# A clustering layer with a 1x1 convolution: the convolution's products in halves of 256 columns, and a changed order in the fourth slot and the last ones

## The chip, the cores and the metric

The kernel runs on one core of one Trainium2 chip. The metric is the device time of one execution in microseconds (us). Three runs of the kernel before took 430.16, 430.51 and 432.31 us; their median is 430.51 us.

## The reference

The input x is 8 x 512 x 32 x 48, that is 8 batches of 512 channels and 1536 tokens. W is 512 x 512, and there are 40 centroids of 512 channels. All is float32.

```
xn  = x / max(norm(x over channels), eps)       cn = centroids / max(norm, eps)
idx = argmax over the 40 centroids of <xn, cn>  onehot = one_hot(idx, 40)
sum_x = onehot^T x ;  count = sum(onehot)       mean = sum_x / max(count, 1)
delta = mean[idx] - x
alpha = exp(-mean over channels of delta^2)
y     = x + alpha * delta
out   = relu(W y + b)
```

The means are taken within a batch, so a batch's tokens must all be assigned before its first delta can be made.

## The kernel before

The work is cut into 24 units of 512 tokens, three per batch. A unit g passes through these steps, each on the engine named:

- **TensorE (PE)**: `similarities` (centroids by x), `transpose_sims`, `sum_clusters` (one-hot by transposed x), `transpose_onehot`, `add_halves`; `gather(g, h)` multiplies means by one-hot and gives the mean of each token in two halves of 256 channels; `sum_squares(g)` sums delta squared over channels into the bank `al` with a matrix of ones; `convolve(g, o)` makes 128 output channels (o = 0 to 3) into one bank of `main` (bank o % 2).
- **VectorE (DVE)**: `transpose_half` transposes x (tile `xs` into `xt`), two instructions per unit; `delta(g, h)`, `add_squares`, `fold`, `low_sum`, `scale(g, h)` (delta times alpha). For the last units also half of y and of its low part.
- **ScalarE (ACT)**: `square`, `move_upper`, `high_sum`, `exp`, `high_half`, `relu(g, o)` (empties the bank of `main`), and small copies.
- **GpSimd (POOL)**: `y_half` (adds x) and `low_half` (y minus its rounded part).

The convolution is made exact enough by splitting both factors. y = YH + YL, W = WH + WL, all of type fp32r, and three products are summed: WH·YH, WH·YL, WL·YH. So `convolve(g, o)` makes 4 values of k times 3 products = 12 matmuls, each with 128 x 128 weights and 512 moving columns, all added into one bank. Each matmul loads its weights first; the load is an instruction of its own, in the profile as PEld. Of the 96 pairs (g, o) two (g = 0, o = 0 and 1) are made elsewhere (L863 to L868 and L909 to L913), which leaves 94 calls.

The order of every engine is written out by hand, and semaphores tie the engines together. A pass through the loop `for g in range(PARTS, UNITS)` is called a slot here: in slot g the unit g gets its delta and its sum of squares, unit g-1 its alpha, y, YH and YL, and unit g-2 is convolved. The slots run from g = 3 to 23; the slot g = 3 is the fourth unit's ("fourth slot"). `beside` is true while a next batch is prepared beside the current one (g < 21); in slots 21 to 23 it is false. After the loop units 22 and 23 are convolved.

Waits that matter below:

- `convolve(g, o)` waits for `relu_done >= 4 g + o - 1` (L818), that is for the relu that emptied its bank; for o = 0 also for YH and YL of the two halves (L822, L823), the second of them only at k = 2.
- `sum_squares(g)` waits for `high_sum(g)` and `low_sum(g)` (L804, L805); `low_sum` itself waits for `high_sum`, and that for `fold` (L538).
- `gather(g, 0)` waits for the last sum of `add_squares(g-1)`, `gather(g, 1)` for `delta(g, 0)` (L791, L796).
- SyncE's queue is in order too: `load_xs(g)` waits for the transposes of unit g-2 (L212), and the loads and stores behind it wait with it (L233 to L246).

Of the kernel before, what the change touches and what calls it, by code (L numbers as in the profile page):

```python
# [16 lines left out]
KC = C // P  # L17
UNIT = 512
PARTS = HW // UNIT
# [46 lines left out]
def build(nc, x, cent, w, bias, out):  # L66
# [3 lines left out]
    with ctx:  # L70
# [16 lines left out]
        YH = [sb(f"yh{j}", [P, KC, UNIT], F32R) for j in range(2)]  # L87
        YL = [sb(f"yl{j}", [P, KC, UNIT], F32R) for j in range(2)]
# [214 lines left out]
        def _(dve):  # L303
# [6 lines left out]
            def transpose_half(g, h):  # L310
                M = C // BLK
                blocks = slice(h * M // 2, (h + 1) * M // 2)
                if h == 0:
                    dve.wait_ge(xs_in[g % 2], 16 * Q * ((g - PARTS) // 2 + 1))
                    dve.wait_ge(c_done, g - PARTS + 1)
                last = v_.transpose(XT[:, g % PARTS, :, :].rearrange("p t (m j) -> p m t j", j=BLK)[:, blocks, :, :],  # L316
                                    XS[g % 2][:, blocks, :])
                if h == 1:
                    last.then_inc(tr_done, 1)

            def best_sims(b):
                dve.wait_ge(simT_done, b + 1)
                wait(dve, oh_done, b)
                v_.tensor_reduce(best[:, :], simT, AXIS_X, ALU.max).then_inc(arg_step, 1)
# [44 lines left out]
            def delta(g, h):  # L369
                dve.wait_ge(gat_done, 2 * g + h + 1)  # L370
                if g >= 2:
                    wait_low(dve, g - 2, h)
                v_.tensor_tensor(Z[g % 2][:, pair(h), :], banks(g, h)[:, :, :],  # L373
                                 X[g // PARTS % 2][:, pair(h), span(g)], ALU.subtract).then_inc(z_done, 1)
# [14 lines left out]
            def low_sum(g):  # L389
                dve.wait_ge(sh_done, folded(g))  # L390
                v_.tensor_tensor(SHL[LOW:P, :], al[0:LOW, :], SHL[0:LOW, :].bitcast(F32), ALU.subtract  # L391
                                 ).then_inc(sl_done, 1)

            def scale(g, h):
                dve.wait_ge(exp_done, g + 1)
                z = Z[g % 2][:, pair(h), :]
                v_.tensor_tensor(z, z, alpha(g).unsqueeze(1).to_broadcast([P, 2, UNIT]), ALU.mult  # L397
                                 ).then_inc(za_done, 1)
# [8 lines left out]
            def low_half(g, h):  # L407
                if not low_on_vector(g, h):
                    return
                dve.wait_ge(hi_done, 2 * g + h + 1)  # L410
                wait(dve, main_done, KC * (g - 1))
                v_.tensor_tensor(YL[g % 2][:, pair(h), :], Z[g % 2][:, pair(h), :],
                                 YH[g % 2][:, pair(h), :].bitcast(F32), ALU.subtract).then_inc(lo_dve, 1)
# [58 lines left out]
            parts_of_mean(1)  # L472
            fold(2)
            low_sum(2)
            transpose_half(6, 0)
            transpose_half(6, 1)
            for g in range(PARTS, UNITS):
                b, p = divmod(g, PARTS)
                beside = b + 1 < BATCH
                delta(g, 0)  # L480
                scale(g - 1, 0)
                scale(g - 1, 1)
                delta(g, 1)
                y_half(g - 1, 1)
                if beside and p < 2:
                    transpose_half(g + 4, 0)
                if beside and p == 2:
                    low_clusters(b + 1)
                    counts(b + 1)
                add_squares(g)  # L490
                if beside and p == 0:
                    transpose_half(g + 4, 1)
                fold(g)
                if beside and p == 2:
                    rest_of_mean(b + 1)
                if beside and p == 1:
                    best_sims(b + 1)
                low_half(g - 1, 1)
                low_sum(g)
                if beside and p == 1:  # L500
                    first_best(b + 1)
                    transpose_half(g + 4, 1)
                if beside and p == 2:
                    parts_of_mean(b + 1)
                    if g + 4 < UNITS:
                        transpose_half(g + 4, 0)
                        transpose_half(g + 4, 1)
            g = UNITS - 1
# [6 lines left out]
        def _(act):  # L515
# [17 lines left out]
            def move_upper(g):  # L533
                act.wait_ge(s_done, folded(g))
                a_.activation(upper_sum[:, :], al[LOW:P, :], ACT.Copy).then_inc(upper_done, 1)  # L535

            def high_sum(g):
                act.wait_ge(fold_done, folded(g))  # L538
                wait(act, one_done, g)
                a_.activation(SHL[0:LOW, :], al[0:LOW, :], ACT.Copy).then_inc(sh_done, 1)  # L540

            def exp(g):
                act.wait_ge(one_done, g + 1)
                a_.activation(alpha(g), alpha(g), ACT.Exp, scale=-1.0 / C).then_inc(exp_done, 1)  # L544

            def high_half(g, h):
                wait_y(act, g, h)
                wait(act, main_done, KC * (g - 1))
                a_.activation(YH[g % 2][:, pair(h), :], Z[g % 2][:, pair(h), :], ACT.Copy).then_inc(hi_done, 1)  # L549

            def relu(g, o):
                if g < 0:
                    return
                act.wait_ge(main_done, KC * g + o + 1)
                if o == 0:
                    wait(act, out_done[g % 2], 16 * (g // 2))
                a_.activation(OUT[g % 2][:, o, :], main[:, o % 2, :], ACT.Relu, bias=bcol[:, o:o + 1]  # L557
                              ).then_inc(relu_done, 1)
# [93 lines left out]
            high_means(1)  # L652
            move_upper(2)
            high_half(1, 1)
            high_sum(2)
            relu(0, 2)
            for g in range(PARTS, UNITS):
                b, p = divmod(g, PARTS)
                beside = b + 1 < BATCH
                relu(g - 3, 3)  # L660
                if g > PARTS:
                    exp(g - 1)
                square(g, 0)
                if beside and p == 2:
                    high_half(g - 1, 0)
                    copy_sums(b + 1)
                    evacuate_onehot(b + 1)
                    square(g, 1)
                    high_half(g - 1, 1)
                    relu(g - 2, 0)  # L670
                    scale_means(b + 1)
                    move_upper(g)
                    high_means(b + 1)
                    high_sum(g)
                    relu(g - 2, 1)
                else:
                    relu(g - 2, 0)
                    if g == PARTS:
                        exp(g - 1)
                    square(g, 1)  # L680
                    if beside:
                        copy_sims(3 * b + 3 + 2 * p)
                    high_half(g - 1, 0)
                    if beside and p == 0:
                        copy_sims(3 * b + 4)
                    if not beside:
                        relu(g - 2, 1)
                    move_upper(g)
                    high_half(g - 1, 1)
                    high_sum(g)  # L690
                    if beside:
                        relu(g - 2, 1)
                relu(g - 2, 2)
                if beside and p == 1:
                    copy_onehot(b + 1)
# [13 lines left out]
        def _(pe):  # L709
# [98 lines left out]
            def sum_squares_direct(g):  # L808
# [4 lines left out]
                                     start=(k == 0), stop=(k == KC - 1))  # L813
                last.then_inc(one_done, 1)

            def convolve(g, o, ks=range(KC)):
                if ks[0] == 0:
                    wait(pe, relu_done, KC * g + o - 1)  # L818
                rows = slice(o * P, (o + 1) * P)
                for k in ks:  # L820
                    if o == 0 and k % 2 == 0:
                        pe.wait_ge(hi_done, 2 * g + k // 2 + 1)  # L822
                        wait_low(pe, g, k // 2)  # L823
                    t_.matmul(main[:, o % 2, :], WH[:, k, rows], YH[g % 2][:, k, :], start=(k == 0), stop=False)  # L824
                    t_.matmul(main[:, o % 2, :], WH[:, k, rows], YL[g % 2][:, k, :], start=False, stop=False)  # L825
                    last = t_.matmul(main[:, o % 2, :], WL[:, k, rows], YH[g % 2][:, k, :], start=False,  # L826
                                     stop=(k == KC - 1))
                if ks[-1] == KC - 1:
                    last.then_inc(main_done, 1)

# [141 lines left out]
```

## Time and profile before

| | |
|---|---|
| median of three runs | 430.51 us |
| the profiled execution | 429.74 us, of which the span of the trace is 427.9 us |
| granted TensorE clock | 1.00 of 2.4 GHz |
| PE busy (matmuls) | 416.4 us, 97% |
| PEld busy (weight loads) | 291.1 us, 68% |
| DVE, ACT, POOL busy | 301.8, 255.1, 206.6 us |
| mean of one, DVE | transpose 1.23, delta 1.22, scale 1.21, low_half 1.37 us |
| mean of one, ACT | high_half 1.05, relu 0.68, exp 0.59, high_sum 0.59 us |
| mean of one, POOL | y_half 2.39, low_half 2.42 us |

The span runs from the first to the last instruction; 1.8 us of the execution lie around it. Rows of the trace have the start in us, the duration in us, the engine, the line, the operation, the tiles (output <- inputs) and shapes, a count of equal instructions that stand in a row, and in brackets the idle time of the engine ahead of it with what ended it. The record of a matmul is longer than the time by which the next one follows, since matmuls overlap in the array; the pace is read from the starts. "x8" rows cover eight records, and their duration is from the first start to the last end. A float32 matmul (f32, not fp32r) stands in the trace as two records, each of two passes over its columns.

### The profile page before, as it was taken

What the parts mean: (1) busy time and instruction counts of PE and PEld (TensorE: products, weight loads), DVE (VectorE), ACT (ScalarE), POOL (GpSimd) and SP (SyncE); (2) the same over time, 40 slices, a digit from 0 to 9 for tenths busy, and PEclk for the clock granted to TensorE, in tenths of its full rate; (3) what the DMA queues carried; (4) which work ended last, traced back from release to release, by engine and by line L of the source; (5) the groups of instructions that cost most, each with busy time, mean ns of one, the idle gap of its engine ahead of it and who ended that gap; (6) DMA issues with size and microseconds to landing.
All of it is one profiled execution on the core that took longest, in us unless ns stands there. A gap on an engine that the chain in (4) does not pass through costs nothing.

```text
span 427.9 us, 5755 instructions
## 1 busy us (share of the span) xinstructions
PE 416.4 (97%) x2106; PEld 291.1 (68%) x2106; DVE 301.8 (71%) x400; ACT 255.1 (60%) x351; POOL 206.6 (48%) x102
## 2 busy tenths in 40 slices
PE   7999998899999999999999999999999999999996
PEld 6744464675867757775767758777677758777785
DVE  2468977687884868678694877958685877788730
ACT  5755383665764675656755666647745657566641
POOL 2000653774563771854744853735816745324320
DMA  8997296867489393966769573983946220222213
GB/s 276 309 285 129 59 266 162 256 192 179 165 207 284 100 243 105 281 159 164 230 164 251 176 185 114 256 232 121 272 90 205 100 98 2 98 100 98 94 68 133
DMA packets 70927, 73.94 MB, mean 173 GB/s; under 512 B 2724, under 2 KB 45732, under 8 KB 70900
## 3 DMA queue, kind: packets, MB, share of 16 engines
q1 hardware_dynamic: 70900, 73.58, 61.6%
q8 instruction: 17, 0.28, 0.3%
q14 instruction: 10, 0.08, 0.1%
HBM read 48.40 MB, written 25.17 MB: 172 GB/s over the span
## 4 chain that ended last, share of the span: by engine, by line
PE 81%; DVE 10%; ACT 3%; issue 2%; DMA 2%; SPq 0%; ACTq 0%; DVEq 0%
PE main L824 17%; PE main L825 16%; PE main L826 16%; PE sump L768 10%; PE fa L728 8%; PE gat L799 5%; DVE z L397 2%; DMA x<-x 2%; DVE z L373 2%; DVE xt L316 1%; PE al L806 1%; PE fa L737 1%; PE fa L752 1%; PE main L867 1%; DVE al L383 1%
## 5 line engine op out<-in xcount | busy, mean ns | idle before, releaser
L286 POOL TENSOR_TENSOR z<-z,x 128x1024 f32<-128x1024 f32 x42 | 99.4, 2386 | 144.8 <-DVE z L397 144.8
L824 PE MATMUL main<-yh,wh 128*128 128x512 f32 x376 | 152.5, 406 | 2.9 <-ACT o L557 2.9
L826 PE MATMUL main<-yh,wl 128*128 128x512 f32 x376 | 146.7, 390 | 0.0
L825 PE MATMUL main<-yl,wh 128*128 128x512 f32 x376 | 146.7, 390 | 0.0
L293 POOL TENSOR_TENSOR yl<-z,yh 128x1024 fp32r<-128x1024 f32 x44 | 105.9, 2423 | 58.6 <-ACT yh L549 58.6
L557 ACT ACTIVATE o<-main,bcol 128x512 f32<-128x512 f32 x96 | 65.1, 682 | 70.9 <-PE main L826 70.9
L373 DVE TENSOR_TENSOR z<-gat,x 128x1024 f32<-128x1024 f32 x46 | 56.2, 1222 | 59.3 <-PE gat L799 59.3
L824 PEld LDWEIGHTS main<-yh,wh 128*128 128x128 f32 x376 | 70.6, 188 | 23.8 <-issue 4.6
L826 PEld LDWEIGHTS main<-yh,wl 128*128 128x128 f32 x376 | 70.6, 188 | 15.2
L825 PEld LDWEIGHTS main<-yl,wh 128*128 128x128 f32 x376 | 70.7, 188 | 13.9
L549 ACT ACTIVATE yh<-z 128x1024 fp32r<-128x1024 f32 x48 | 50.4, 1051 | 22.9 <-POOL z L286 21.9
L397 DVE TENSOR_TENSOR z<-z,al 128x1024 f32<-128x1024 f32 x46 | 54.0, 1213 | 3.5 <-ACT al L544 3.5
L316 DVE STREAM_TRANSPOSE xt<-xs 128x1024 f32<-128x1024 f32 x42 | 51.0, 1230 | 0.0
L728 PE MATMUL fa<-x,c_t 128*64 128x256 f32 x384 | 45.2, 383 | 0.6 <-DMA x<-x 0.3
L768 PE MATMUL sump<-xt,oh 128*64 128x512 f32 x192 | 43.6, 598 | 0.0
L728 PEld LDWEIGHTS fa<-x,c_t 128*64 128x64 f32 x384 | 26.7, 137 | 18.0 <-issue 6.9
L531 ACT ACTIVATE gat<-z 128x1024 f32<-128x1024 f32 x22 | 22.6, 1027 | 20.6 <-DVE z L373 20.6
L531 ACT ACTIVATE sq<-z 128x1024 f32<-128x1024 f32 x22 | 23.3, 1061 | 16.3 <-DVE z L373 16.3
L768 PEld LDWEIGHTS sump<-xt,oh 128*64 128x64 f32 x192 | 12.8, 136 | 25.5 <-issue 25.5
L799 PE MATMUL gat<-oht,g 128*128 128x512 bf16 x92 | 27.8, 384 | 1.1 <-DVE g L366 0.6
L387 DVE TENSOR_TENSOR al<-upper_sum,al 64x512 f32<-64x512 f32 x22 | 15.0, 680 | 10.2 <-ACT upper_sum L535 10.2
L391 DVE TENSOR_TENSOR shl<-al,shl 64x512 fp32r<-64x512 f32 x22 | 15.1, 685 | 6.8 <-ACT shl L540 6.5
(114 smaller groups left out, 335.7 us busy)
## 6 DMA issues: line engine op xcount, KB each, us to landing
x<-x SPq DMA_DIRECT2D x24, 1024.0 KB, 5.7
out<-o SPq DMA_DIRECT2D x23, 1024.0 KB, 5.6
xs<-x SPq DMA_DIRECT2D x84, 256.0 KB, 5.6
o<-w SPq DMA_DIRECT2D x1, 1024.0 KB, 12.2
out<-o SPq DMA_DIRECT2D x4, 256.0 KB, 2.1
sq<-centroids SPq DMA_DIRECT2D x2, 80.0 KB
bcol<-bias SPq DMA_DIRECT2D x1, 2.0 KB, 11.8
```

The costliest lines, as they stand in the source:

```text
L286: pool.tensor_tensor(z, z, X[g // PARTS % 2][:, pair(h), span(g)], ALU.add).then_inc(y_pool, 1)
L293: pool.tensor_tensor(YL[g % 2][:, pair(h), :], Z[g % 2][:, pair(h), :], YH[g % 2][:, pair(h), :].bitcast(F32), ALU.subtract).then_inc(lo_p ...
L316: last = v_.transpose(XT[:, g % PARTS, :, :].rearrange("p t (m j) -> p m t j", j=BLK)[:, blocks, :, :], XS[g % 2][:, blocks, :])
L373: v_.tensor_tensor(Z[g % 2][:, pair(h), :], banks(g, h)[:, :, :], X[g // PARTS % 2][:, pair(h), span(g)], ALU.subtract).then_inc(z_done, 1)
L397: v_.tensor_tensor(z, z, alpha(g).unsqueeze(1).to_broadcast([P, 2, UNIT]), ALU.mult).then_inc(za_done, 1)
L549: a_.activation(YH[g % 2][:, pair(h), :], Z[g % 2][:, pair(h), :], ACT.Copy).then_inc(hi_done, 1)
L557: a_.activation(OUT[g % 2][:, o, :], main[:, o % 2, :], ACT.Relu, bias=bcol[:, o:o + 1]).then_inc(relu_done, 1)
L728: last = t_.matmul(simP[u][NPAD * h:NPAD * (h + 1), :], cT[:, k, :], toks, start=(k == 0), stop=(k == KC - 1))
L768: last = t_.matmul(sumP[NPAD * h:NPAD * (h + 1), :], oh[:, slot(u, tile), :], XT[:, u, tile, :], start=(u == 0 and t == 0), stop=(u == PAR ...
L824: t_.matmul(main[:, o % 2, :], WH[:, k, rows], YH[g % 2][:, k, :], start=(k == 0), stop=False)
L825: t_.matmul(main[:, o % 2, :], WH[:, k, rows], YL[g % 2][:, k, :], start=False, stop=False)
L826: last = t_.matmul(main[:, o % 2, :], WL[:, k, rows], YH[g % 2][:, k, :], start=False, stop=(k == KC - 1))
```

## The change

Two things are changed.

**Halves.** In `convolve` each of the three products of a k is made as two matmuls of 256 columns with the same weights, except WH·YH of k = 0, the first into its bank, which stays 512 wide. A call then makes 1 + 2 + 2 + 3 x 6 = 23 matmuls instead of 12. No weight load is shared: each matmul has its own.

**Orders.** In slot 3: VectorE makes `delta(3, 0)` ahead of the two transposes of unit 6; ScalarE makes `relu(0, 2)` and `relu(0, 3)` ahead of `high_sum(2)` instead of behind it. In slots 21 to 23: ScalarE makes `high_sum(g)` ahead of `high_half(g-1, 1)`; VectorE makes `low_sum(g)` ahead of `low_half(g-1, 1)` (in the other slots VectorE has no `low_half`, so that edit moves nothing there).

```
             for g in range(PARTS, UNITS):
                 delta(g, 0)
+                if g == PARTS:
+                    transpose_half(g + 3, 0)
+                    transpose_half(g + 3, 1)
...
+                low_sum(g)
                 low_half(g - 1, 1)
-                low_sum(g)
...
             high_half(1, 1)
+            relu(0, 2)
+            relu(0, 3)
             high_sum(2)
-            relu(0, 2)
...
                     move_upper(g)
+                    if not beside:
+                        high_sum(g)
                     high_half(g - 1, 1)
-                    high_sum(g)
                     if beside:
+                        high_sum(g)
                         relu(g - 2, 1)
...
-                    t_.matmul(main[:, o % 2, :], WH[:, k, rows], YH[g % 2][:, k, :], start=(k == 0), stop=False)
-                    t_.matmul(main[:, o % 2, :], WH[:, k, rows], YL[g % 2][:, k, :], start=False, stop=False)
-                    last = t_.matmul(main[:, o % 2, :], WL[:, k, rows], YH[g % 2][:, k, :], start=False,
-                                     stop=(k == KC - 1))
+                    if k == 0:
+
+                        t_.matmul(main[:, o % 2, :], WH[:, k, rows], YH[g % 2][:, k, :], start=True, stop=False)
+                    else:
+                        for half in column_halves:
+                            t_.matmul(main[:, o % 2, half], WH[:, k, rows], YH[g % 2][:, k, half],
+                                      start=False, stop=False)
+                    for half in column_halves:
+                        t_.matmul(main[:, o % 2, half], WH[:, k, rows], YL[g % 2][:, k, half],
+                                  start=False, stop=False)
+                    for half in column_halves:
+                        last = t_.matmul(main[:, o % 2, half], WL[:, k, rows], YH[g % 2][:, k, half],
+                                         start=False, stop=(k == KC - 1 and half is column_halves[-1]))
```

VectorE around the start of slot 3, before: L387 and L391 are `fold(2)` and `low_sum(2)`, L316 the transposes of unit 6, L373 `delta(3, 0)`, L397 `scale(2, 0)` and `scale(2, 1)`.

```order
53 L387 TENSOR_TENSOR al<-upper_sum,al 64x512
54 L391 TENSOR_TENSOR shl<-al,shl 64x512
55 L316 STREAM_TRANSPOSE xt<-xs 128x8x4x32 x2
56 L373 TENSOR_TENSOR z<-gat,x 128x1024
57 L397 TENSOR_TENSOR z<-z,al 128x1024 x2
```

And now:

```order
53 L387 TENSOR_TENSOR al<-upper_sum,al 64x512
54 L391 TENSOR_TENSOR shl<-al,shl 64x512
55 L373 TENSOR_TENSOR z<-gat,x 128x1024
56 L316 STREAM_TRANSPOSE xt<-xs 128x8x4x32 x2
57 L397 TENSOR_TENSOR z<-z,al 128x1024 x2
```

The two transposes now stand between the delta and the scaling.

ScalarE in slot 22, before: L535 is `move_upper`, L549 `high_half`, L540 `high_sum`, L557 `relu`.

```order
272 L557 ACTIVATE o<-main,bcol 128x512
273 L535 ACTIVATE upper_sum<-al 64x512
274 L549 ACTIVATE yh<-z 128x1024
275 L540 ACTIVATE shl<-al 64x512
276 L557 ACTIVATE o<-main,bcol 128x512 x2
```

And now (the same functions stand one line lower in the changed file):

```order
272 L558 ACTIVATE o<-main,bcol 128x512
273 L536 ACTIVATE upper_sum<-al 64x512
274 L541 ACTIVATE shl<-al 64x512
275 L550 ACTIVATE yh<-z 128x1024
276 L558 ACTIVATE o<-main,bcol 128x512 x2
```

The copy that `low_sum` waits for has moved ahead of one of 1.05 us.

TensorE in one call of `convolve`, now: L832 is the wide product of k = 0, L835, L838 and L841 are WH·YH, WH·YL and WL·YH in halves.

```order
747 L832 MATMUL main<-yh,wh 128x512
748 L838 MATMUL main<-yl,wh 128x256 x2
749 L841 MATMUL main<-yh,wl 128x256 x2
750 L835 MATMUL main<-yh,wh 128x256 x2
751 L838 MATMUL main<-yl,wh 128x256 x2
752 L841 MATMUL main<-yh,wl 128x256 x2
```

Eleven of a call's twelve matmuls have become pairs.

## Rows read from the trace of the kernel before

**Rows 1.** The page's parts 1 and 4: busy time, and the chain that ended last.

```profile
PE 416.4 (97%) x2106; PEld 291.1 (68%) x2106; DVE 301.8 (71%) x400; ACT 255.1 (60%) x351; POOL 206.6 (48%) x102
PE 81%; DVE 10%; ACT 3%; issue 2%; DMA 2%; SPq 0%; ACTq 0%; DVEq 0%
```

**Rows 2.** Windows: busy time of each engine in one stretch, clock, DMA share, GB/s.

```profile
118.00:365.00 247.00, 247.00 (x1258) 173.54 (x1257) 182.08 (x219) 152.23 (x210) 141.84 (x60) 1.00 0.63 175
```

**Rows 3.** Timeline of TensorE at the end: from one row to the other are 48 matmuls.

```profile
413.44 0.39 PE L826 MATMUL main<-yh,wl 128*128 128x512 f32 x1
...
424.32 0.39 PE L826 MATMUL main<-yh,wl 128*128 128x512 f32 x1
```

**Rows 4.** Timeline of TensorE: float32 matmuls of 512 columns, bf16 transposes of 128.

```profile
37.73 3.60 PE L812 MATMUL al<-o,ones 128*128 128x512 f32 x8
41.16 3.60 PE L812 MATMUL gat<-o,ones 128*128 128x512 f32 x8
...
57.19 0.83 PE L752 MATMUL fa<-identb,oh 128*128 128x128 bf16 x12
```

**Rows 5.** Lines L825 and L799: duration of one record, min/median/max in ns.

```profile
L825 PEld LDWEIGHTS main<-yl,wh x376: 187/188/192, 57.9 to 423.9; 128*128 128x128 f32 x188
L825 PE MATMUL main<-yl,wh x376: 387/389/398, 58.1 to 424.1; 128*128 128x512 f32 x188
...
L799 PE MATMUL gat<-oht,g x92: 377/379/390, 33.4 to 393.7; 128*128 128x512 bf16 x92
```

**Rows 6.** The costliest groups: line L752; behind the bar busy us and mean ns.

```profile
L752 PE MATMUL fa<-identb,oh 128*128 128x128 bf16 x96 | 6.7, 219 | 0.0
```

**Rows 7.** Timeline of all engines at 205.4: weight loads at a convolution's start.

```profile
205.47 0.19 PEld L824 LDWEIGHTS main<-yh,wh 128*128 128x128 f32 x1
205.58 0.19 PEld L825 LDWEIGHTS main<-yl,wh 128*128 128x128 f32 x1
...
205.81 0.39 PE L825 MATMUL main<-yl,wh 128*128 128x512 f32 x1
```

**Rows 8.** The same at 88.0: a convolution's last matmul and the gather behind it.

```profile
88.01 0.39 PE L826 MATMUL main<-yh,wl 128*128 128x512 f32 x1
...
88.24 0.12 PEld L799 LDWEIGHTS gat<-oht,g 128*128 128x128 bf16 x2 [0.26 <-issue]
```

**Rows 9.** Timeline of TensorE in slot 3.

```profile
64.80 0.61 PE L799 MATMUL gat<-oht,g 128*128 128x512 bf16 x2 [0.33 <-DVE g L366]
66.58 0.50 PE L824 MATMUL main<-yh,wh 128*128 128x512 f32 x1 [1.18 <-ACT o L557]
...
81.96 0.50 PE L824 MATMUL main<-yh,wh 128*128 128x512 f32 x1 [1.76 <-ACT o L557]
```

**Rows 10.** Timeline of ScalarE in slot 3.

```profile
63.10 1.05 ACT L549 ACTIVATE yh<-z 128x1024 fp32r<-128x1024 f32 x1
65.37 0.59 ACT L540 ACTIVATE shl<-al 64x512 fp32r<-64x512 f32 x1 [1.22 <-DVE al L387]
65.86 1.25 ACT L557 ACTIVATE o<-main,bcol 128x512 f32<-128x512 f32 x2
70.22 1.06 ACT L531 ACTIVATE sq<-z 128x1024 f32<-128x1024 f32 x1 [3.11 <-DVE z L373]
```

**Rows 11.** Timeline of VectorE in slot 3.

```profile
66.71 2.37 DVE L316 STREAM_TRANSPOSE xt<-xs 128x1024 f32<-128x1024 f32 x2
69.00 1.19 DVE L373 TENSOR_TENSOR z<-gat,x 128x1024 f32<-128x1024 f32 x1
72.38 2.35 DVE L397 TENSOR_TENSOR z<-z,al 128x1024 f32<-128x1024 f32 x2 [2.19 <-ACT al L544]
```

**Rows 12.** Timeline of the SyncE queue: the loads behind the transposes of unit 6.

```profile
69.11 1.91 SPq L215 DMA_DIRECT2D xs<-x  x4
```

**Rows 13.** Timeline of TensorE in slot 21, at the end of unit 19's convolution.

```profile
376.85 0.39 PE L826 MATMUL main<-yh,wl 128*128 128x512 f32 x1
...
377.45 0.47 PE L806 MATMUL al<-shl,ones 128*128 128x512 f32 x1 [0.22 <-DVE shl L391]
```

More of the change, by code:

```diff
@@ L474, in _ @@
             low_sum(2)
-            transpose_half(6, 0)
-            transpose_half(6, 1)
             for g in range(PARTS, UNITS):
@@ L659, in _ @@
                 beside = b + 1 < BATCH
-                relu(g - 3, 3)
                 if g > PARTS:
+                    relu(g - 3, 3)
                     exp(g - 1)
@@ L814, in sum_squares_direct @@
                 last.then_inc(one_done, 1)
+            column_halves = (slice(0, UNIT // 2), slice(UNIT // 2, UNIT))
             def convolve(g, o, ks=range(KC)):
```

## The prediction

> **What bounds the kernel now.** I read the page's busy times and its chain first, then windows, then the timeline of TensorE. The reader is to see that PE is busy for 97% of the span and makes 81% of the chain [rows 1], and that from 118 to 365 us it is busy for all of 247.00 us while no other engine passes 182 us [rows 2]. So in the middle a matmul that gets longer or shorter moves the end by the same amount, and an order moves nothing. Orders can pay only where PE has gaps: in slot 3, and a little in slots 21 to 23 [rows 9, 13].
>
> **The halves: how many.** 94 calls of `convolve` make eleven pairs each, which is 94 x 11 = 1034 pairs. So the answer is 1034 times what a pair of 256 columns costs more or less than one matmul of 512. 10 ns in a pair are 10.3 us.
>
> **What a matmul of 512 costs now.** In the quiet end 48 matmuls take 424.32 - 413.44 = 10.88 us, that is 226.7 ns each [rows 3]. 512 columns at the granted 2.4 GHz are 213.3 ns. The float32 matmuls of 512 columns, which also load weights of 128 x 128, take (41.16 - 37.73) / 8 = 428.8 ns for two passes, 214.4 ns a pass [rows 4]. A fp32r matmul is thus some 12 ns slower than a pass of the same columns in float32. The records say the same: 389 ns against 379 ns for bf16 of 512 columns [rows 5]. Where do the 12 ns come from? Not from the next weight load beside it: the gather's load begins 0.23 us after the convolution's last matmul [rows 8], so nothing was loaded beside that matmul, and it still took the full time.
>
> **What a half can cost.** Two things bound it. The stream: 256 columns are 106.7 ns. The loads: every half waits for its own weights. At a convolution's start the loads of the first two matmuls begin at 205.47 and 205.58, 110 ns apart, though each record is 190 ns [rows 7]; that is how soon one load can follow another when no long stream stands between. In bf16 such records overlap as well: twelve transposes, 219 ns each, follow each other by (830 - 219) / 11 = 56 ns [rows 4, 6], which also shows that PE takes a load and a matmul every 56 ns from its queue, so twice as many instructions at 110 ns don't bind. From these rows a pair can cost:
>
> - 2 x 106.7 = 213.3 ns, if neither loads nor the extra count: a gain of 13.3 ns, 13.8 us in all. The lower bound.
> - 2 x 110 = 220 ns, if the loads set the pace and the extra 12 ns does not come with a short stream: a gain of 6.7 ns, 6.9 us.
> - 226.7 ns, if the extra is a share of the columns (6% more per column): no change.
> - 2 x (106.7 + 13.3) = 240 ns, if the extra is a fixed cost of each fp32r matmul: a loss of 13.3 ns, 13.8 us.
> - 2 x 188 = 376 ns, if a load had to end its record before the next begins [rows 5]: a loss of 154 us. Against it, a second load begins 80 ns before the first record's end [rows 7]. I keep it as the far upper bound, with next to no chance.
>
> I take 220 to 221 ns, that is a gain of 6.2 us, the value nearest to that distance of loads [rows 7]. The reason for choosing it over 226.7: the extra shows in no float32 stream of 512 columns [rows 4], though that reads the same four bytes per column (if at half the rate), so a plain price per column is not what the rows show; and over 240: a price per matmul would be a price per record, and bf16 and float32 records have none. Neither reason is strong. No fp32r matmul of another width than 512 stands in this trace, and this is where I choose.
>
> The trace shows weight loads beside a running stream of the same rows: the load for the matmul at 205.81 began at 205.58, behind the start of the matmul ahead. The Trainium skill ("TensorE: Matmul & The Clock Gate", Part 3, The mechanism) says that a load runs beside matmuls in flight only where it is for other row groups, or goes to the background weight buffer as the same section also has it. By the first of the two a pair would pay a second load of about 107 ns (the page's figure, columns over 1.2 GHz, section LDWEIGHTS), an estimate of +110 us in all, to which I give no chance: the trace, with 226.7 ns for a load and 512 columns, agrees with the second. The same page (Back-to-back issue gap) gives N / 2.4 + 2.5 ns, 215.8 for 512 columns and 109.2 for 256: the first is not what fp32r shows here, the second would be an estimate of 218.3 ns for a pair.
>
> **Slot 3.** PE stands still before `convolve(1, 0)` (1.18 us, for `relu(0, 2)`) and before `convolve(1, 3)` (1.76 us, for `relu(1, 1)`) [rows 9]. First edit: ScalarE is free at 64.15 after `high_half(1, 1)` and now makes the two relus there, not from 65.86 on; `relu(0, 2)` ends at about 64.8. The gather ends at 65.26, so `convolve(1, 0)` starts at 65.3 and not at 66.58, 1.3 us earlier. Its second half (k = 2) needs POOL's low part, which starts behind the same `high_half` at 64.2 and takes 2.4 us (the table's mean): ready at 66.6, when six matmuls are done, so about 0.1 us is lost. The price of the edit is that `high_sum(2)` waits for `relu(0, 3)`, which ends at about 65.4, where it began at 65.37 before [rows 10]: nothing.
>
> Second edit: `delta(3, 0)` starts at 66.7 behind `low_sum(2)`, not at 69.00 [rows 11], 2.3 us earlier; the transposes (2.37 us) take the time to 70.2. The chain behind it: `square(3, 0)` at 67.95 (before: 70.22), `relu(1, 0)` at about 68.95, `exp(2)` at 69.5, `scale(2, 0)` at 70.2 instead of 72.38. That is 2.2 us earlier, and the transposes end just then, so they are hidden. All that ends the second wait (scaling, `delta(3, 1)`, squares, sums, `fold`, `high_sum`, `relu(1, 1)`) follows that scaling in unchanged order, so `convolve(1, 3)` comes at 79.8 instead of 81.96. PE is there sooner and still waits, since its own work up to there moves by some 2.0 us too. The two edits give 2.2 us together and not 1.3 + 2.2: one chain ends both waits.
>
> What is moved along: the transposes of unit 6 end at 70.2 and not at 69.1, and SyncE's four loads for unit 8 wait for them [rows 12], with the first store and the load of x for unit 8 behind. Unit 8 is transposed in slot 4, some 15 us later. I cost it at nothing; if that cover were gone, it would be 1 us.
>
> **Slots 21 to 23.** In slot 21 the last matmul of unit 19 starts at 376.85, and `sum_squares` could follow 0.23 us later, at 377.08; it starts at 377.45 [rows 13], 0.37 us late, for `low_sum`. The new order takes `high_half` (1.05 us) on ScalarE and `low_half` (1.2 us) on VectorE out of its way, so it is ready about 0.9 us sooner and the wait goes. The two moved behind it are needed at k = 2 of the next convolution, over 1.5 us behind the sum, and are then ready. Slots 22 and 23 show the same pair of rows. Three times 0.37 us are 1.1 us. Bounds: 0 and 1.1 us.
>
> **The sum.** -6.2 (halves) - 2.2 (slot 3) - 1.1 (slots 21 to 23) = -9.5 us. The profiled execution took 429.74 us (span 427.9 and 1.8 around it) and would take 420.2. The median of the runs is 0.8 us above it, so the forecast is 430.5 - 9.5 = 421.0 us.
>
> **The rivals.** *The halves cost nothing and give nothing.* A pair takes 226.7 to 229 ns: only the orders count, 427.2 us, or up to 429.6 us if each half has 1 ns more. For it: most fp32r records are at 389 ns but some reach 398 [rows 5], as a stream would that is short of data; that would be a price per column. Against it: the float32 rows.
>
> *A fixed price per fp32r matmul.* This is the one that ends slower: each of the 1034 added matmuls pays 13.3 ns for itself, +13.8 - 3.3 = +10.5, so 441.0 us. It decides from the point where a pair costs more than 226.7 + 3.3 / 1034 us = 229.9 ns: above that the time rises. For it: 226.7 ns are 544 cycles, 512 and 32, and one width can't tell a fixed 32 from a share. Against it: nothing of the kind in the other types.
>
> *The stream alone counts.* The loads are hidden, and a half has the pace of the float32 passes, half of 214.4 plus about a ns: a pair at 218 to 218.5, 418.5 us. For it: [rows 4]. Against it: the 110 ns between loads.
>
> *The orders don't do what they say*, for instance because unit 6's transposes or the first store come late: then 3 us of the sum are missing in whatever case holds, 424 us in the likeliest.
>
> **How the numbers follow.** Loads set the pace (421.0): 0.36, of which a tenth with the orders failing. Stream alone (418.5): 0.14. No change from the halves: 0.29; two thirds of it below 428.3. Fixed price: 0.17. Something dearer or cheaper by a mishap, as a clock that falls: 0.04. What a measurement of this kernel can tell from no change is about 0.5%, 2.2 us, so faster means below 428.3 and slower above 432.7. Faster: 0.36 + 0.14 + 0.20 = 0.70. Same: 0.09 + 0.02 = 0.11. Slower: 0.17 + 0.02 = 0.19. The range 417.5 to 432 leaves out the fixed price and the mishaps; the likeliest case alone has 419.5 to 424.
>
> **What would show it.** Halves: starts of convolution matmuls 110 ns apart (right), 113 (no change), 120 (fixed price); weight loads starting at the same distances. Slot 3: `convolve(1, 0)` 1.3 us sooner behind its gather, `convolve(1, 3)` 2.2 us sooner, `exp(2)` behind a square that begins near 68 us. Slots 21 to 23: `sum_squares` 0.23 us behind the last half, no wait for VectorE. The forecast is wrong if the distance between halves is above 113 ns, whatever the orders do.

## The result, and the profile after

The changed kernel takes 438.13 us (median of 4 runs, 437.86 to 438.45), the kernel before 430.34 us: the ratio is 1.018 (95% interval 1.0151 to 1.0205). It is 7.8 us slower, where 9.5 us faster were forecast, and outside the range of 417.5 to 432 us. Both parts of the sum can be read from the trace after. First the page, its parts 1 and 4, beside [rows 1]; the last row is part 5's for the product WH·YL (the second number behind the bar is the mean length of one record in ns).

```profile
PE 428.4 (98%) x3140; PEld 349.6 (80%) x3140; DVE 301.9 (69%) x400; ACT 254.9 (58%) x351; POOL 206.8 (47%) x102
...
PE 91%; DVE 4%; ACT 2%; DMA 1%; issue 1%; POOL 1%; SPq 0%; DVEq 0%
...
L838 PE MATMUL main<-yl,wh 128*128 128x256 f32 x752 | 151.5, 283 | 0.0
```

PE has 3140 - 2106 = 1034 matmuls more, as counted. The other engines do what they did. Now the timeline of TensorE near the end, for [rows 3]:

```profile
427.75 0.40 PE L838 MATMUL main<-yl,wh 128*128 128x256 f32 x2
...
430.15 0.40 PE L841 MATMUL main<-yh,wl 128*128 128x256 f32 x2
```

Between these starts lie ten pairs (only halves): 2.40 us, 240 ns a pair, 120 ns a half. Forecast were 220 ns, and one matmul of 512 columns took 226.7. The records of the weight loads (190 ns) overlap, as [rows 7] let expect, and their busy time rose by 58.5 us only.

In slot 3 the orders did what was forecast. The timeline of TensorE, for [rows 9]:

```profile
65.33 0.61 PE L803 MATMUL gat<-oht,g 128*128 128x512 bf16 x2
...
80.24 0.50 PE L832 MATMUL main<-yh,wh 128*128 128x512 f32 x1 [1.04 <-ACT o L558]
83.20 0.40 PE L810 MATMUL al<-shl,ones 128*128 128x512 f32 x1
```

From the gather of the slot to `convolve(1, 3)` it takes 14.91 us, before 81.96 - 64.80 = 17.16 us: 2.25 us less, with 2.2 forecast. The wait ahead of `convolve(1, 0)` is gone. And the sums of squares of slots 20 and 23, for [rows 13]:

```profile
372.27 0.40 PE L810 MATMUL al<-shl,ones 128*128 128x512 f32 x1
...
410.05 0.39 PE L810 MATMUL al<-shl,ones 128*128 128x512 f32 x1
```

In the trace before, the same two stand at 365.02 and 402.45, and that of slot 3 at 84.81:

```profile
84.81 0.40 PE L806 MATMUL al<-shl,ones 128*128 128x512 f32 x1
...
365.02 0.40 PE L806 MATMUL al<-shl,ones 128*128 128x512 f32 x1
...
402.45 0.47 PE L806 MATMUL al<-shl,ones 128*128 128x512 f32 x1 [0.20 <-DVE shl L391]
```

So slots 21 to 23 take 37.78 us and took 37.43. The slots between (from the sum of squares of slot 3, at 84.81 before and 83.20 after, to that of slot 20) take 289.07 us and took 280.21: 8.86 us more for 17 slots x 44 = 748 pairs, 11.8 ns a pair.

That is less than the 240 - 226.7 = 13.3 ns of the quiet end, because in the middle the matmul of 512 columns was slower than 226.7 ns already in the kernel before. Its timeline of TensorE:

```profile
209.72 0.40 PE L825 MATMUL main<-yl,wh 128*128 128x512 f32 x1
...
212.00 0.39 PE L826 MATMUL main<-yh,wl 128*128 128x512 f32 x1
```

Ten matmuls lie between these starts, 228 ns each, which is also the mean from 118 to 365 us. In the changed kernel a pair has 239.5 ns in the mean of the same stretch. What adds the 1.3 ns in the middle is open.

### The profile page after: what moved, and what is told of

It reads as the page before. It is cut to its first block, busy times and chain, and to the rows that moved or that the text cites. A ratio compares the mean times of both kernels' runs of the same rounds, so it can differ in the third digit from the quotient of the medians.

```text
span 436.7 us, 7823 instructions
## 1 busy us (share of the span) xinstructions
PE 428.4 (98%) x3140; PEld 349.6 (80%) x3140; DVE 301.9 (69%) x400; ACT 254.9 (58%) x351; POOL 206.8 (47%) x102
## 4 chain that ended last, share of the span: by engine, by line
PE 91%; DVE 4%; ACT 2%; DMA 1%; issue 1%; POOL 1%; SPq 0%; DVEq 0%
PE main L838 20%; PE main L841 20%; PE main L835 15%; PE sump L772 10%; PE fa L732 9%; PE main L832 5%; PE gat L803 5%; DVE xt L316 1%; DMA x<-x 1%; PE fa L741 1%; PE al L810 1%; PE fa L756 1%; PE main L882 1%; PE al L816 1%; PE gat L816 1%
## 5 line engine op out<-in xcount | busy, mean ns | idle before, releaser
L838 PE MATMUL main<-yl,wh 128*128 128x256 f32 x752 | 151.5, 283 | 0.0
L841 PE MATMUL main<-yh,wl 128*128 128x256 f32 x752 | 151.5, 283 | 0.0
L838 PEld LDWEIGHTS main<-yl,wh 128*128 128x128 f32 x752 | 123.1, 190 | 4.9
L841 PEld LDWEIGHTS main<-yh,wl 128*128 128x128 f32 x752 | 116.7, 190 | 0.0
L835 PE MATMUL main<-yh,wh 128*128 128x256 f32 x564 | 113.5, 283 | 0.0
L373 DVE TENSOR_TENSOR z<-gat,x 128x1024 f32<-128x1024 f32 x46 | 56.3, 1223 | 67.3 <-PE gat L803 67.3
L835 PEld LDWEIGHTS main<-yh,wh 128*128 128x128 f32 x564 | 87.4, 190 | 0.2
L397 DVE TENSOR_TENSOR z<-z,al 128x1024 f32<-128x1024 f32 x46 | 54.0, 1213 | 1.1 <-ACT al L545 1.1
L316 DVE STREAM_TRANSPOSE xt<-xs 128x1024 f32<-128x1024 f32 x42 | 51.0, 1229 | 0.0
L832 PE MATMUL main<-yh,wh 128*128 128x512 f32 x94 | 43.0, 457 | 1.0 <-ACT o L558 1.0
L832 PEld LDWEIGHTS main<-yh,wh 128*128 128x128 f32 x94 | 17.8, 190 | 8.2 <-issue 4.6
```

What stands on the lines that cost most here:

```text
L835: t_.matmul(main[:, o % 2, half], WH[:, k, rows], YH[g % 2][:, k, half], start=False, stop=False)
L838: t_.matmul(main[:, o % 2, half], WH[:, k, rows], YL[g % 2][:, k, half], start=False, stop=False)
L841: last = t_.matmul(main[:, o % 2, half], WL[:, k, rows], YH[g % 2][:, k, half], start=False, stop=(k == KC - 1 and half is column_halves[-1]))
```

## The experiments

**The orders without the halves** (`orders_only`): the changed kernel with `convolve` of the kernel before.

> The kernel before with the order edits of slot 3 and of slots 21 to 23, and every product 512 columns wide. Both theories of the halves say the same here: all of the loss of the changed kernel is the halves', and the orders give what the prediction gave them, 2.2 + 1.1 = 3.3 us: 427.1 us, ratio 0.9925. If the orders failed as one rival has it: 430.3 us. In the trace: convolve(1, 0) behind its gather without a wait, and sum_squares of slots 21 to 23 at 0.23 us behind the last matmul.

Measured: 426.31 us, ratio 0.9908 (0.9894 to 0.9922). The orders gain 4.0 us (3.4 to 4.6 by the interval), a little more than the 3.3 expected; in the two traces the stretch from the gather of slot 3 to its sum of squares is 2.2 us shorter and slots 21 to 23 are 1.3 us shorter, 3.5 in all. Both signs are there: `convolve(1, 0)` has no wait, and `sum_squares` starts 0.23 us behind the last matmul (374.82 and 375.05).

**The halves without the orders** (`halves_only`): the kernel before with `convolve` of the changed one.

> The kernel before with the halves and without any order edit. If the two parts add up: 438.1 + 3.3 = 441.4 us, ratio 1.026. If the orders gave nothing, 438.1 us. The time of a slot between two sums of squares should be that of the changed kernel (15.2 us mean) from slot 4 to 21.

Measured: 440.86 us, ratio 1.0241 (1.022 to 1.0262): the halves cost 10.5 us. From the sum of squares of slot 3 to that of slot 20 it takes 289.08 us, the changed kernel 289.07. That is 17.0 us a slot; the 15.2 of the expectation was a slip. The 441.4 us expected of parts that add up lie within the interval, so the end time alone doesn't decide whether they do. The parts add up to 10.5 - 4.0 = 6.5 us, and the change costs 7.8. The difference of 1.3 us is what slots 21 to 23 show. The timeline of TensorE of `halves_only`, the same two sums of squares:

```profile
376.41 0.40 PE L806 MATMUL al<-shl,ones 128*128 128x512 f32 x1
...
414.19 0.39 PE L806 MATMUL al<-shl,ones 128*128 128x512 f32 x1
```

37.78 us, to the hundredth what the changed kernel has with the new orders, and neither row has a wait in brackets. With halves PE is slower by about 0.5 us a slot, `low_sum` is no longer late, and the order edit of these slots is worth nothing. In `orders_only` they take 36.14 us (363.00 to 399.14), 1.29 less than before.

**One product in halves** (`one_product`): of the three products only this is changed against `orders_only`.

```
-                    t_.matmul(main[:, o % 2, :], WH[:, k, rows], YL[g % 2][:, k, :], start=False, stop=False)
+                    for half in column_halves:
+                        t_.matmul(main[:, o % 2, half], WH[:, k, rows], YL[g % 2][:, k, half],
+                                  start=False, stop=False)
```

> The orders of the changed kernel, but only the product WH*YL in halves: 94 x 4 = 376 matmuls more than before instead of 1034. Theory A, a fixed price of each fp32r matmul (10.6 ns net each, as the slots of the changed kernel show): 427.1 + 376 x 10.6 ns = 431.1 us. Theory B, the second load can't keep up with two short matmuls in a row but a long one behind them lets the loads catch up: the price of a pair next to wide matmuls is less than half of it, under 429.1 us.

Measured: 431.25 us, ratio to before 1.0026 (1.0011 to 1.004), and 4.9 us over `orders_only`: 13.1 ns for each of 376 matmuls. That fits theory A, whose 4.0 us came from 10.6 ns each (with the 11.8 of the slots it would be 4.4); a load that catches up behind wide matmuls (B) would have shown less than 2 us. The single distances are another matter. The timeline of TensorE near the end:

```profile
412.89 0.40 PE L832 MATMUL main<-yl,wh 128*128 128x256 f32 x2
413.12 0.40 PE L834 MATMUL main<-yh,wl 128*128 128x512 f32 x1
...
413.59 0.39 PE L832 MATMUL main<-yl,wh 128*128 128x256 f32 x2
```

The two halves take 230 ns together, less than the 240 of theory A, and each of the two wide matmuls behind them 233 ns, more than its 226.7. The three products take 697 ns in the mean where three wide ones take 680. So the price is there in the sum, but beside another width a start does not stand where a price of 13.3 ns for each matmul puts it; why is open.

**The widths** (`widths`): behind the last `convolve`, series such as

```
+            for i in range(24):
+                t_.matmul(gat[:, 0, 0:256], WH[:, kk(i), col(i)], y[:, kk(i), 0:256], start=True, stop=True)
```

> The kernel before with 13 series of 24 matmuls behind the last convolution, whose results nobody reads; the time is read per series, not in all. Theory A (each fp32r matmul pays some 13 ns beside its columns, whatever the width): starts 226.7 ns apart for 512 columns, 173 for 384, 120 for 256; with weights of 64 columns the same 226.7 and 120. Theory B (no such price, weight loads set the pace of 256 columns at 120 ns): 384 columns 162 to 170 ns, 128 and 64 columns 120 ns as well, and with weights of 64 columns the 256 column series goes at 107 to 110 ns. Rival C, a share of 6% of the columns: 170 ns for 384, 113 for 256 columns. bf16 in all theories: 216, 109, 56 ns for 512, 256, 128 columns; float32: 429 and 216 ns for 512 and 256 columns (two passes each).

The timeline of TensorE. A row's duration runs from the first start to the last end.

```profile
424.27 5.60 PE L956 MATMUL gat<-yh,wh 128*128 128x512 f32 x24
429.71 4.35 PE L958 MATMUL gat<-yh,wh 128*128 128x384 f32 x24
433.90 3.03 PE L960 MATMUL gat<-yh,wh 128*128 128x256 f32 x24
436.76 2.80 PE L962 MATMUL gat<-yh,wh 128*128 128x128 f32 x24
439.39 2.81 PE L964 MATMUL gat<-yh,wh 128*128 128x64 f32 x24
442.04 5.71 PE L966 MATMUL gat<-yh,wh 128*64 128x512 f32 x24
447.59 2.89 PE L968 MATMUL gat<-yh,wh 128*64 128x256 f32 x24
450.55 5.13 PE L970 MATMUL gat<-oht,g 128*128 128x512 bf16 x23
455.51 2.78 PE L972 MATMUL gat<-oht,g 128*128 128x256 bf16 x24
458.13 1.50 PE L974 MATMUL gat<-oht,g 128*128 128x128 bf16 x24
...
480.13 10.52 PE L978 MATMUL gat<-x,ident 128*128 128x256 f32 x48
490.30 5.84 PE L980 MATMUL gat<-yh,wh 128*128 128x512 f32 x24
```

The distance of starts is the distance of one row to the next over 24: fp32r with 512 columns (429.71 - 424.27) / 24 = 227 ns, 384 columns (433.90 - 429.71) / 24 = 175 ns (median 173), 256 columns 119 ns, 128 columns 110 ns (median 111), 64 columns 110 ns (median 112). Over the 2.4 GHz columns (213.3, 160, 106.7) that is 13 ns each time for 512, 384 and 256: a price per matmul, not per column. At 128 and 64 columns the distance no longer falls with the columns; it stays at 110 to 112 ns, the distance of loads in [rows 7]. At 256 the matmuls keep 120, above that distance. bf16 with 256 columns takes (458.13 - 455.51) / 24 = 109 ns. A float32 record of 256 columns, which is two passes, takes 216 ns (median), 2.5 more than its 512 columns at 2.4 GHz. (The Trainium skill, "TensorE: Matmul & The Clock Gate", section Back-to-back issue gap, has N / 2.4 + 2.5 ns, 109.2 for 256 columns: the bf16 series agrees, the float32 series does if its two passes count as one matmul of 512 columns, the fp32r series does not.) Theory A holds for weights of 128 columns; B and C fall. With weights of 64 columns the picture is mixed: with 512 moving columns the distance was (447.59 - 442.04) / 24 = 231 ns (median 229), no less than before, but with 256 moving ones 113 ns where A said 120. There the price is about half, and A has no reason for it. So it is not excluded that at 256 columns a part of the 13 ns is the load's.

**The operands** (`sources`): series of 256 columns with one thing changed in each.

> The kernel before with 12 series of 24 fp32r matmuls (256 columns, one series 320) behind the last convolution, each changed in one thing. Theory A1 (the 13 ns belong to the type, whatever the operands are): 117 to 120 ns in every series, 147 ns for 320 columns, and where fp32r and bf16 matmuls take turns a pair takes at least 120 + 107 ns. Theory A2 (they belong to the path of one operand): the series that changes that operand (64 rows, other tile, same weights, other bank, accumulation, weights of 32 columns) falls to 113 ns or less and the others stay.

```profile
434.35 3.04 PE L962 MATMUL gat<-yh,wl 128*128 128x256 f32 x24
437.23 3.04 PE L964 MATMUL gat<-yh,wh 128*128 128x256 f32 x24
440.11 3.04 PE L966 MATMUL gat<-yh,wh 128*128 128x256 f32 x24
442.99 3.04 PE L968 MATMUL gat<-yh,wh 128*128 128x256 f32 x24
445.87 3.04 PE L970 MATMUL gat<-yh,wh 128*128 128x256 f32 x24
448.75 3.04 PE L972 MATMUL gat<-wh 128*128 128x256 f32 x24
451.63 0.28 PE L974 MATMUL gat<-yh,wh 128*128 128x256 f32 x1
...
461.02 2.88 PE L979 MATMUL gat<-yh,wh 128*32 128x256 f32 x24
```

Each of the first six begins 2.88 us ahead of the next, 120.0 ns a matmul: the low weights, the same weights each time, the upper 256 columns, banks in turn, accumulation, another moving tile. The medians of 64 rows and of the low factor moving are 120 as well, 320 columns have 147. Only weights of 32 columns fall to 113 ns, (2.88 - 0.28) / 23. In the series in which fp32r and bf16 matmuls take turns a pair takes 244 ns, where A1 asked for at least 227. A1 holds for all but the narrow weights, and A2 is right in this one point. What makes the second half of the price with weights of 128 columns, the load or the array, is not settled.

**Slot 3 in pieces** (`relus_only`, `slot3_only`).

> The kernel before with one order edit alone, relu(0, 2) and relu(0, 3) ahead of high_sum(2). Theory of the prediction (one chain through delta(3, 0), the square, exp(2) and the scaling ends the second wait): convolve(1, 0) starts right behind its gather, 1.2 us sooner than before, but convolve(1, 3) does not come sooner, and from the gather of slot 3 to its sum of squares it takes 20.0 us as before (gain 0 to 0.1 us). Rival (PE's own work moves the rest): 1.2 us less, 18.8 us.

> The kernel before with both edits of slot 3 and none of slots 21 to 23. From the gather of slot 3 to its sum of squares 17.6 us instead of 20.0, as in the kernel with all orders; slots 21 to 23 take 37.4 us between the sums of squares of slots 20 and 23, as before, where the kernel with all orders has 36.1.

The timeline of TensorE of `relus_only`:

```profile
65.67 0.61 PE L800 MATMUL gat<-oht,g 128*128 128x512 bf16 x2 [0.33 <-DVE g L366]
...
71.20 0.59 PE L800 MATMUL gat<-oht,g 128*128 128x512 bf16 x2 [1.74 <-DVE z L373]
...
82.83 0.50 PE L825 MATMUL main<-yh,wh 128*128 128x512 f32 x1 [1.76 <-ACT o L557]
```

`convolve(1, 0)` starts without a wait, but the second gather waits 1.24 us longer for `delta(3, 0)` (1.74 against 0.50), and from gather to `convolve(1, 3)` it takes 17.16 us, as before. So the relus alone only move a wait, as one chain for both waits says. `slot3_only` (427.58 us in one execution) has, in the same view,

```profile
64.88 0.60 PE L801 MATMUL gat<-oht,g 128*128 128x512 bf16 x2 [0.33 <-DVE g L366]
68.55 0.61 PE L801 MATMUL gat<-oht,g 128*128 128x512 bf16 x2
79.79 0.50 PE L826 MATMUL main<-yh,wh 128*128 128x512 f32 x1 [1.36 <-ACT o L558]
```

14.91 us, 2.25 less; its sum of squares then comes at 82.67, 17.8 us behind the gather (17.6 expected), and slots 21 to 23 take 37.43 us as before. The edit of VectorE without the relus was not run.

In the one execution of `relus_only` (432.22 us) TensorE's granted clock fell to half behind the two waits. From the gather to the sum of squares it took 21.6 us, where 20.0 were expected. The next run asks whether that belongs to the edit.

> The same kernel as relus_only (the two relus moved, nothing else), timed. In its one look slot 3 gained nothing and TensorE's granted clock fell to half at the end of the slot, which cost 1.6 us. If the fall comes with this order each time: about 432 us, ratio 1.004. If it was of that one execution: 430.1 us, ratio 1.000.

429.90 us, ratio 0.9985 (0.9966 to 1.0005), with the same two waits and the clock at 1.00 in the profiled execution: the fall does not come with the order each time, and the edit alone is worth nothing that can be measured.

**One edit more** (`orders_relu`): `orders_only`, and in slot 3 also

```
-                    if not beside:
+                    if not beside or g == PARTS:
                         relu(g - 2, 1)
                     move_upper(g)
```

with the later `relu(g - 2, 1)` left out in that slot.

> The kernel with all order edits and 512 column products, and one edit more: in slot 3 relu(1, 1) ahead of move_upper(3), not behind high_sum(3). Theory (ScalarE's order alone holds convolve(1, 3) back, since relu(1, 1) could run at 76.9 us): the wait of 1.4 us goes, less what the sum of squares then lacks; 424.9 to 425.3 us. Rival (the sum of squares of slot 3 becomes late by what ScalarE lost): 426.0 us or more.

Measured: 424.98 us, ratio 0.9878 (0.9861 to 0.9894). ScalarE's timeline:

```profile
76.45 0.47 ACT L569 ACTIVATE sims<-fa,cstat 128x256 f32<-128x256 f32 x1
76.81 0.69 ACT L558 ACTIVATE o<-main,bcol 128x512 f32<-128x512 f32 x1
77.52 0.60 ACT L536 ACTIVATE upper_sum<-al 64x512 f32<-64x512 f32 x1
```

The relu runs at 76.81, and `convolve(1, 3)` no longer waits. This kernel is faster than both: 5.1 us under the one before, 13.2 under the changed one.

## Why the prediction was wrong

- **The count** was right: 1034 pairs, and where PE has no waits the end moves by what a pair costs. The middle slots show it.
- **The cost of a half** was the step that failed. I took "the value nearest to that distance of loads", 220 to 221 ns for a pair; it is 240, and in the middle slots a pair costs 11.8 ns more than one matmul of 512. The term was -6.2 us and measures +10.5. The load's pace of 110 ns was read rightly (128 columns go at 111), but in the series it was a floor and not the time of 256 columns. The reasons for passing over the fixed price were weak in different ways. That float32 streams show no extra spoke only against a price per column of any data; the price is tied to the type, so "bf16 and float32 records have none" said nothing of fp32r (they have 2.5 ns a record). The one fact of fp32r in the trace was 226.7 ns at one width, which a share and a constant fit alike. Nothing in it spoke for an extra that vanishes in a short stream, and the forecast rested on just that. In the first rival, 1 ns more in each half is 2.1 us and gives 429.3 us; the 429.6 belongs to a pair of 229 ns.
- **The rival** "a fixed price per fp32r matmul" is what happened, with a chance of 0.17: some 13 ns for 512, 384 and 256 columns where the weights have 128. Its 441.0 us were 2.9 us high. Some 1.1 us of this is the middle, where 748 pairs cost 11.8 ns and not 13.3. More of it is in slot 3 and in slots 21 to 23, where a slower PE first used up its own waits: the three last slots hold 132 pairs, and took 0.35 us more, where the rival's own terms (132 x 13.3 ns less 1.1 us) make 0.66. The rest is not traced.
- **Slot 3** was right in size (2.25 for 2.2 us), and the mechanism, one chain for both waits, fits: the first edit alone gives 0, both give all.
- **Slots 21 to 23** were right alone (1.3 for 1.1 us; behind a sum of squares that had waited the gather also started later, 0.32 us after it at 377.45 in the kernel before and 0.24 us after it at 397.46 in the changed one), and wrong beside the halves, where they give 0. I had added the terms as if each stood alone. With halves that gain they might have; with halves that cost they could not.
- **The loads, the queue, the transposes of unit 6 and SyncE's loads** were costed at nothing, and no new wait of PE shows there.

## What to carry to other kernels

When a matmul's time lies above its columns over the clock, one width can't tell a price per column from a price per matmul, and other types don't tell it for this one: a series of two or more widths does, and until it is run, cutting a matmul in two should be expected to pay whatever is fixed twice. A distance between loads was a lower bound here, not a forecast. A gain from a wait is only there while the wait is, so edits that slow the waiting engine eat it.

## What the runs showed of the hardware

In series of one width a fp32r matmul with 128 weight columns took its columns at 2.4 GHz and 13 to 14 ns more (227, 173, 147 and 120 ns for 512, 384, 320 and 256 columns). At 256 columns it was 120 ns whatever moved and whatever bank it wrote. bf16 took 2.5 ns more than its columns (216 and 109 ns for 512 and 256) and float32 2.5 ns for two passes (429 and 216 ns). At the lower of the two clocks, 1.2 GHz, the price was gone. The windows of `relus_only` (the last three numbers are the granted clock, the DMA share and GB/s):

```profile
85.00:88.00 3.00, 3.00 (x10) 2.02 (x10) 0.00 (x0) 0.51 (x1) 0.00 (x0) 0.62 1.21 210
88.00:91.00 3.00, 3.00 (x15) 2.15 (x13) 2.83 (x3) 1.80 (x4) 0.40 (x1) 1.00 0.93 285
```

and its timeline of TensorE:

```profile
85.56 0.63 PE L827 MATMUL main<-yh,wl 128*128 128x512 f32 x1
...
86.84 0.61 PE L827 MATMUL main<-yh,wl 128*128 128x512 f32 x1
```

Three matmuls lie between these starts, 427 ns apart, which is 512 columns at 1.2 GHz with nothing added. The engine had waited 1.74 us up to 71.20 and 1.76 us up to 82.83. The same two waits (1.72 and 1.76 us) stand in the profiled execution of `relus_timed`, where the clock stayed at 2.4 GHz, so the waits alone don't decide it. Nor does the edit: three of the 13 executions of the kernel before that ran beside `relus_timed` had the same mean clock as `relus_only`, 0.996, and took 432.10 to 432.25 us; where in them the clock was lower is not known.

A bf16 load behind a fp32r matmul was not made ahead. The timeline of all engines in `sources`, where the two took turns with 256 columns each:

```profile
451.79 0.36 PE L974 MATMUL gat<-yh,wh 128*128 128x256 f32 x1
451.99 0.10 PEld L975 LDWEIGHTS gat<-oht,g 128*128 128x128 bf16 x1
452.00 0.28 PE L975 MATMUL gat<-oht,g 128*128 128x256 bf16 x1
```

The bf16 load begins 0.20 us behind the start of the fp32r matmul, just ahead of its own matmul. A pair took 244 ns, 15 ns more than 120 + 109.
